# Attention scores by matmuls of 32-row groups in place of zero-padded 104-row ones

## The reference

```
h, hd = 16, 8
q, k, v = x @ Wq, x @ Wk, x @ Wv              # split into 16 heads of 8
log_f = log_sigmoid(x @ Wf);  c = cumsum(log_f)
scores = q k^T * hd**-0.5 + c[i] - c[j]       # causal
out = softmax(scores) @ v;   x += out @ Wo
```

## Time and profile before

| | us |
|---|---|
| median of 3 runs (533.71 to 541.26) | 535.29 |
| span of the profiled execution | 528.3 |
| PE busy, 3680 matmuls | 454.1 (86%) |
| PE weight loads | 320.7 (61%) |
| DVE busy | 377.8 (72%) |
| ACT busy | 278.7 (53%) |
| POOL busy | 148.2 (28%) |

### The profile page before, as it was taken

How to read it: one execution, slowest core, us unless ns; L and a number is a source line. 1 busy time by engine, 2 the same in 40 slices (tenths; PEclk the granted TensorE clock), 3 DMA queues, 4 the chain that set the end, 5 groups by cost and what they waited for, 6 DMA issues and landing times.

```text
span 528.3 us, 12106 instructions
## 1 busy us (share of the span) xinstructions
PE 454.1 (86%) x3680; PEld 320.7 (61%) x3680; DVE 377.8 (72%) x1348; ACT 278.7 (53%) x757; POOL 148.2 (28%) x235
## 2 busy tenths in 40 slices
PE   1788887767989899999999999999999988888884
PEld 1666665554656576576676676676676656666662
DVE  3999999767566576576675675675665654999996
ACT  3477675422445455455455456456355655676663
POOL 8856655421011010110110110110110001556644
PEclk9999999768899999999999999999999999999999
DMA  4210000133322323313312412413312000000101
GB/s 124 80 30 2 1 0 1 63 109 107 101 78 69 110 61 81 113 58 80 115 56 80 115 55 81 117 52 82 115 56 80 5 3 1 20 23 20 40 22 40
DMA packets 30173, 32.31 MB, mean 61 GB/s; under 512 B 3262, under 2 KB 26910, under 8 KB 30140
## 3 DMA queue, kind: packets, MB, share of 16 engines
q1 hardware_dynamic: 30140, 31.92, 21.1%
HBM read 16.05 MB, written 15.20 MB: 59 GB/s over the span
## 4 chain that ended last, share of the span: by engine, by line
PE 33%; DVE 24%; DMA 16%; issue 10%; SPq 8%; POOL 6%; ACT 1%; DVEq 1%; POOLq 0%
DMA a_q_rows<-a_max_t 12%; DVE m_lower L275 6%; PE bank L807 6%; PE bank L790 6%; PE bank L775 6%; SPq L571 4%; PE bank L793 3%; PE bank L778 2%; DVE a_neg_c L757 2%; PE bank L891 2%; POOL a_c_parts L613 2%; DVE a_neg_max L690 2%; POOL a_c_parts L611 2%; DVE x_all L284 2%; DVE m_stats L302 2%
## 5 line engine op out<-in xcount | busy, mean ns | idle before, releaser
L690 DVE TENSOR_REDUCE a_neg_max<-bank 128x2 f32<-128x512 f32 (+1 forms) x192 | 125.5, 686 | 103.5 <-PE bank L778 101.8
L634 ACT ACTIVATE a_weights<-bank 128x512 f32<-128x512 f32 x192 | 105.0, 589 | 82.5 <-PE bank L790 41.2
L775 PE MATMUL bank<-a_k_rows,a_q_rows 104*128 104x256 f32 (+1 forms) x512 | 101.9, 324 | 6.4 <-DMA a_k_rows<-k_stage 6.0
L775 PEld LDWEIGHTS bank<-a_k_rows,a_q_rows 104*128 104x128 f32 x512 | 80.1, 201 | 25.2 <-issue 16.6
L790 PE MATMUL bank<-a_q_rows,a_k_rows 106*128 106x512 f32 x192 | 78.2, 481 | 18.4 <-DMA a_q_rows<-a_max_t 17.1
L238 ACT ACTIVATE m_scaled<-bank,m_gates 128x128 f32<-128x128 f32 x256 | 72.3, 365 | 27.0 <-PE bank L384 27.0
L611 POOL TENSOR_TENSOR a_c_parts<-a_neg_c,a_zero_row 16x256 fp32r<-16x256 f32 x16 | 11.5, 720 | 219.2 <-DVE a_neg_c L757 219.2
L213 POOL TENSOR_TENSOR m_pair<-m_scaled 128x256 f32<-128x256 f32 x64 | 48.3, 755 | 73.0 <-ACT m_scaled L238 72.9
L275 DVE SCALAR_TENSOR_TENSOR m_lower<-bank,m_gates,m_lower 128x128 f32<-128x128 f32 x192 | 65.5, 341 | 1.3
L778 PE MATMUL bank<-a_mask,a_ident 128*128 128x256 bf16 (+1 forms) x192 | 63.3, 330 | 0.0
L807 PE MATMUL bank<-a_weights,a_v 128*32 128x128 f32 x1536 | 62.1, 280 | 0.0
(11 more groups left out here) (118 smaller groups left out, 838.2 us busy)
## 6 DMA issues: line engine op xcount, KB each, us to landing
a_k_rows<-k_stage SPq DMA_DIRECT2D x16, 416.0 KB
k_stage<-a_k_parts SPq DMA_DIRECT2D x48, 128.0 KB
q_stage<-a_q_parts SPq DMA_DIRECT2D x48, 128.0 KB
a_q_rows<-q_stage SPq DMA_DIRECT2D x64, 96.0 KB
x_all<-in_L_attn_x SPq DMA_DIRECT2D x8, 256.0 KB, 2.8
out_x<-x_all SPq DMA_DIRECT2D x8, 256.0 KB, 2.3
a_q_rows<-a_max_t SPq DMA_DIRECT2D x64, 8.0 KB, 2.6
we<-in_L_ffn_We SPq DMA_DIRECT2D x1, 512.0 KB, 4.1
```

Source lines behind the costliest of these rows:

```text
L634: nc.scalar.activation(weights[n // 2 % 3][:, half:half + 4, :].rearrange("p h n -> p (h n)"), wt_bank[n % 2][:, :], ACT.Exp).then_inc(wt_ ...
L690: nc.vector.tensor_reduce(neg_max[:, t, first:first + heads], score_bank[p % 2][:, :].rearrange("p (h n) -> p h n", h=heads), AX.X, ALU.ma ...
L775: nc.tensor.matmul(bank[:, n * keys:(n + 1) * keys], q_rows[b][0:KR, h, t * P:(t + 1) * P], k_rows[b][0:KR, h % NU, 0:keys], start=n == 0, ...
```

## The change

Each group of heads gets its own 32 partitions: rows 32g to 32g+23 the parts, then two of ones (q) or of -c (k), then two for the maxima, 28 in all. `q_rows` shrinks from 106 x 16 x 256 to 128 x 4 x 256 and has no zeros; `set_up_rows` goes. Scores are made for two banks at a time: matmuls of group g into one bank and of group g+1 into the other, in turn, and then the two mask matmuls. Turned scores: each of the six pairs of banks gets 8 matmuls of 128 columns in place of 2 of 512, again in turn between two groups. Both wait for both banks where each bank had its own wait. The k rows are loaded by four DMAs, the maxima are spread over four partitions. `normalise`, `times_v` and `row_max` follow the new order of heads.

```diff
-    ROWS = 3 * HD + 2
-    KR = NG * ROWS
-    KM = KR + 2
+    QR, KR, KM = 3 * HD, 3 * HD + 2, 3 * HD + 4
+    row_group = lambda g, rows: slice(32 * g, 32 * g + rows)
...
-    q_rows = [sb(f"q_rows{b}", [KM, H, N], FP32R) for b in range(3)]
-    k_rows = [sb(f"k_rows{b}", [KM, NU, N], FP32R) for b in range(3)]
+    q_rows = [sb(f"q_rows{b}", [P, NU, N], FP32R) for b in range(3)]
+    k_rows = [sb(f"k_rows{b}", [P, NU, N], FP32R) for b in range(3)]
...
-                sp.dma_start(raw(q_rows[s % 3])[KR + part:KR + part + 1, :, t * P:(t + 1) * P],
+                sp.dma_start(raw(q_rows[s % 3])[KR + part:P:32, :, t * P:(t + 1) * P],
                              raw(max_t[t])[:, part, :]).then_inc(max_in[t], 16)
...
-                sp.dma_start(raw(k_rows[b])[0:KR, :, :], k_dram[b].rearrange("g r u n -> (g r) u n")).then_inc(rows_in, 16)
+                for g in range(NG):
+                    sp.dma_start(raw(k_rows[b])[row_group(g, KR), :, :], k_dram[b, g]).then_inc(rows_in, 16)
...
-    def set_up_rows(pool, b):
-
-        nc.gpsimd.memset(q_rows[b][:, :, :].bitcast(U32), 0).then_inc(zeroed, 1)
...
         def scores(i, s, p):
-            at_least(pe, max_done, i * 12 + p - 1)
...
+            at_least(pe, max_done, i * 12 + p)
+            b = s % 3
+            parts = [score_part(p), score_part(p + 1)]
+            t, keys = int(p >= 4), parts[0][1]
+            for n in range(len(parts[0][2])):
+                for bank, (g, _, heads) in zip(score_bank, parts):
+                    u = heads[n]
+                    nc.tensor.matmul(bank[:, n * keys:(n + 1) * keys], q_rows[b][row_group(g, KR), u, t * P:(t + 1) * P],
+                                     k_rows[b][row_group(g, KR), u, 0:keys], start=n == 0, stop=False, skip_group_check=True)
+            for bank, (_, _, heads) in zip(score_bank, parts):
+                own = bank[:, :].rearrange("p (h n) -> p h n", h=len(heads))[:, :, keys - P:keys]
+                nc.tensor.matmul(own, ident16[:, :], mask16[:, 0:len(heads), :], start=False, stop=True,
+                                 skip_group_check=True).then_inc(scores_ready, 1)
+
+        def turned_scores(i, s, k):
...
+            at_least(pe, wt_exp, i * 12 + 2 * k)
+            b = s % 3
+            t, first, jt = (0, 2 * k, 0) if k < 2 else (1, 2 * ((k - 2) // 2), k % 2)
             diagonal = jt == t
...
+            for u in range(NU):
+                for half in range(2):
+                    rows = row_group(first + half, KM)
+                    last = nc.tensor.matmul(wt_bank[half][:, u * P:(u + 1) * P], k_rows[b][rows, u, jt * P:(jt + 1) * P],
+                                            q_rows[b][rows, u, t * P:(t + 1) * P], start=u == 0, stop=not diagonal,
+                                            skip_group_check=True)
+                    if not diagonal and u == NU - 1:
+                        last.then_inc(wt_ready, 1)
             if diagonal:
-                last = nc.tensor.matmul(bank[:, :], ident16[:, :], mask16_t[:, :, :], start=False, stop=True)
-            last.then_inc(wt_ready, 1)
+                for half in range(2):
+                    nc.tensor.matmul(wt_bank[half][:, :], ident16[:, :], mask16_t[:, :, :], start=False, stop=True,
+                                     skip_group_check=True).then_inc(wt_ready, 1)
```

More of the change, by code:

```diff
@@ L518, in attention_layer @@
     k_stored, q_stored, c_stored, w_ordered = sem("k_stored"), sem("q_stored"), sem("c_stored"), sem("w_ordered")
-    LOADS = NG + 1
+    LOADS = 2 * NG
     raw = lambda tile: tile[(slice(None),) * len(tile.shape)].bitcast(FP32)
     q_dram = nc.dram_tensor("q_stage", (3, NG, 3 * HD, NU, N), FP32, kind="Internal").ap()
-    k_dram = nc.dram_tensor("k_stage", (3, NG, ROWS, NU, N), FP32, kind="Internal").ap()
+    k_dram = nc.dram_tensor("k_stage", (3, NG, KR, NU, N), FP32, kind="Internal").ap()
     f_part = lambda s: 2 if s >= 0 else 3
     def constant_rows(sp):
-        sp.wait_ge(zeroed, 4)
+        sp.wait_ge(zeroed, 1)
         ones = ones_r[:, :].bitcast(FP32).rearrange("r (u n) -> r u n", u=NU)
@@ L532, in constant_rows @@
             for g in range(NG):
-                sp.dma_start(raw(q_rows[b])[ROWS * g + 3 * HD:ROWS * (g + 1), NU * g:NU * (g + 1), :], ones).then_inc(ones_in, 16)
-            sp.dma_start(raw(k_rows[b])[KR:KM, :, :], ones).then_inc(ones_in, 16)
+                sp.dma_start(raw(q_rows[b])[32 * g + QR:32 * g + KR, :, :], ones).then_inc(ones_in, 16)
+                sp.dma_start(raw(k_rows[b])[32 * g + KR:32 * g + KM, :, :], ones).then_inc(ones_in, 16)
     def sync(sp):
@@ L552, in step @@
                 for g in range(NG):
-                    sp.dma_start(raw(q_rows[b])[ROWS * g:ROWS * g + 3 * HD, NU * g:NU * (g + 1), :],
-                                 q_dram[b, g]).then_inc(rows_in, 16)
+                    sp.dma_start(raw(q_rows[b])[row_group(g, QR), :, :], q_dram[b, g]).then_inc(rows_in, 16)
                 wait_apart(sp, k_stored, n * 16 * 3, sp_waited)
                 sp.wait_ge(c_stored, n * 16 * 2)
-                sp.dma_start(raw(k_rows[b])[0:KR, :, :], k_dram[b].rearrange("g r u n -> (g r) u n")).then_inc(rows_in, 16)
+                for g in range(NG):
+                    sp.dma_start(raw(k_rows[b])[row_group(g, KR), :, :], k_dram[b, g]).then_inc(rows_in, 16)
             if 0 <= s < NSEQ:
@@ L688, in row_max @@
             dve.wait_ge(scores_ready, i * 12 + p + 1)
-            t, first, heads = (0, 4 * p, 4) if p < 4 else (1, 2 * (p - 4), 2)
+            pair, half = divmod(p - 4, 4)
+            t, first, heads = (0, 4 * p, 4) if p < 4 else (1, NU * (2 * pair + half % 2) + 2 * (half // 2), 2)
             nc.vector.tensor_reduce(neg_max[:, t, first:first + heads],
@@ L704, in normalise @@
             dve.wait_ge(recip_done, i * 2 + t + 1)
[L705 to L708, removed]
+            nc.vector.tensor_tensor(attn[:, t], out[:, :, 0:HD],
+                                    recip[:, t].unsqueeze(2).broadcast_to([P, H, HD]), ALU.mult).then_inc(attn_done, 1)
         def part(i, s, j):
@@ L767, in tensor @@
     def tensor(pe):
-        def scores(i, s, p):
-            at_least(pe, max_done, i * 12 + p - 1)
[L770 to L779, removed]
@@ L781, in turned_scores, with score_part @@
-        def turned_scores(i, s, n):
-            if n == 0:
+        def score_part(p):
+            if p < 4:
+                return p, P, range(NU)
+            pair, half = divmod(p - 4, 4)
+            return 2 * pair + half % 2, 2 * P, range(2 * (half // 2), 2 * (half // 2) + 2)
+        def scores(i, s, p):
+            at_least(pe, max_done, i * 12 + p)
[11 more added lines that the diff above has]
+                                 skip_group_check=True).then_inc(scores_ready, 1)
@@ L783, in turned_scores @@
+        def turned_scores(i, s, k):
+            if k == 0:
                 pe.wait_ge(max_in[0], (i + 1) * 32)
-            if n == 4:
+            if k == 2:
                 pe.wait_ge(max_in[1], (i + 1) * 32)
-            at_least(pe, wt_exp, i * 12 + n - 1)
-            b, bank = s % 3, wt_bank[n % 2]
-            t, u, jt = (0, n, 0) if n < 4 else (1, (n - 4) // 2, n % 2)
+            at_least(pe, wt_exp, i * 12 + 2 * k)
+            b = s % 3
+            t, first, jt = (0, 2 * k, 0) if k < 2 else (1, 2 * ((k - 2) // 2), k % 2)
@@ L789, in turned_scores @@
             diagonal = jt == t
-            last = nc.tensor.matmul(bank[:, :], k_rows[b][0:KM, u, jt * P:(jt + 1) * P],
-                                    q_rows[b][0:KM, u:H:NU, t * P:(t + 1) * P], start=True, stop=not diagonal)
+            for u in range(NU):
[6 more added lines that the diff above has]
+                        last.then_inc(wt_ready, 1)
@@ L803, in times_v @@
             b, w = s % 3, weights[k % 3]
+            t, first, jt = (0, 2 * k, 0) if k < 2 else (1, 2 * ((k - 2) // 2), k % 2)
             for half in range(2):
[L805 to L808, removed]
+                g = first + half
+                for u in range(NU):
+                    last = nc.tensor.matmul(out_bank[t][32 * u:32 * (u + 1), g * P:(g + 1) * P], v_sb[b][:, jt, NU * g + u, :],
+                                            w[:, 4 * half + u, :], start=jt == 0 and g == 0, stop=jt == t,
+                                            skip_group_check=True)
             last.then_inc(av_done, 1)
@@ L828, in part @@
                 pe.wait_ge(set_up, 2)
-                pe.wait_ge(ones_in, 16 * 3 * (NG + 1))
+                pe.wait_ge(ones_in, 16 * 3 * 2 * NG)
                 pe.wait_ge(before["tiles_done"], 2 * NSEQ)
@@ L836, in part @@
                 scores(i, s, 2 * j)
-                scores(i, s, 2 * j + 1)
             if j == 0 and X:
@@ L863, in part @@
             if X:
-                turned_scores(i - 1, s - 1, 2 * j)
-                turned_scores(i - 1, s - 1, 2 * j + 1)
+                turned_scores(i - 1, s - 1, j)
             if j == 3 and T:
@@ L899, in tensor @@
         return part
```

(5 more changed lines are left out.)

## The result

The changed kernel takes 573.9 us (median of 4 runs, 565.0 to 580.9) against 535.7 before: 1.060 times as long, 95% interval 1.049 to 1.071. The profiled one is that of 565.0 us. Its span of 562.3 is 34.0 us above the span before, which had a mean clock of 0.972.

What follows compares the result with a forecast made beforehand. It took the loop through the slow stage writes to the maxima's landing as bound in steady steps, PE elsewhere. Steps +6.2, filling and emptying +2.0, exp +1, start -0.3 gave +8.9 on 535.3: 544 us, range 525 to 588.

Steps and rivals of the forecast that it cites:

- What bounds the kernel: Steady attention step: stage writes on about four DMA engines delay the maxima, 11.6 us from first stage issue to landing.
- The matmuls: Score and turned-score matmuls: two row groups run side by side, load and stream, saving 2.14 us per step.
- rival B: Row groups don't run side by side, or loads queue: PE grows 4.68 us a step, 595 us; chance 0.24.
- The switches: Changes between 32-row tiles and full-array matmuls: 18 new ones per step at 0.15 us, 2.70 us on PE.
- A: The forecast case: 538 us at 0.10 a switch to 552 at 0.20, PE busy 19.3 a step; chance 0.45.
- Rival C: Not slower: going between 32-row and full matmuls needs no drain, below 0.07 us a switch; 526 us, chance 0.26.
- The loop: Way from one landing of maxima to the next: +0.37 us of PE work, +0.15 for the maxima, +0.52 per step.
- -0.30: Turned scores at k = 2: four rounds replace two 512-column matmuls and a mask moved to k = 3, -0.30 us.
- The 0.15 for them: Maxima DMAs written into four partitions, with more small packets: 0.15 us longer, between 0 and 0.3.
- The double waits, D: Waits for both banks bite: exp or second maximum 0.3 us late in most steps, 550 us; chance 0.05.
- the clock: PE's clock in steady steps: falling below 1.0 would spoil the signs to look for; no price or chance given.
- The sum: Whole kernel: steps +6.2, pipeline filling and emptying +2.0, exp +1, start -0.3, together +8.9 us.

Runs made afterwards that it cites:

- Run 9: Kernel before with q and k columns and DRAM stages reordered so stage writes spread, k rows loaded by four DMAs: 0.940, 504.4 us.
- run 1: Changed kernel's order, counts and double waits, but without 32-row tiles: score matmuls contract over 122 or 124 zero-padded rows; 1.058 of the kernel before, 563.0 us.
- run 6: Changed kernel plus four full-array filling matmuls of 512 columns in part j = 2, before the wait for the maxima: 1.030 of the kernel before, 550.3 us.
- run 7: Changed kernel plus four filling matmuls of 512 columns in the same wait, as 32-row tiles over 24 rows: 1.069 of the kernel before, 576.5 us.
- run 4: Changed kernel without any mask matmul, scores and turned scores unmasked: 1.123 of the kernel before, 599.3 us.
- run 5: Kernel before without any mask matmul, scores and turned scores unmasked: 1.011, 543.2 us.
- run 10: Changed kernel with the DRAM stages reordered so that stage writes spread: 0.984 of the kernel before, 528.9 us.
- run 11: Scores alone tiled in 32-row groups, turned scores padded as before, stage writes spread: 0.930 of the kernel before, 497.6 us.
- run 2: Scores alone tiled as in the change, turned scores one 512-column matmul over padded rows: 1.024 of the kernel before, 548.9 us.

## Why the prediction came out as it did

**What bounds the kernel: right.** The distance from SP's first stage issue to the landing was 11.6 us and is 11.5 now (305.72 to 317.21). Run 9 bears it out.

**The matmuls: right.** Two groups run side by side, loads included: 0.055 a turned matmul, against 0.105 in run 1. So rival B, queued loads at 595 us, is refuted. That a round with 256 keys takes 0.115 is carried over from before: four take 0.43 with the switch, which does not part the two.

**The switches: right in the sum, wrong in the split.** With rounds at the prices of before, entering costs 0.43 - 0.23 = 0.20 and 0.59 - 0.40 = 0.19, where the prediction had 0.15; with the 0.11 a round that the loads' starts show, the second is 0.15. Leaving to a mask costs 0.33 - 0.26 = 0.07 and 0.54 - 0.46 = 0.08, where it had 0.15. A pair is 0.27 against 0.30. PE is busy for 18.9 us of a step, where 19.3 was forecast for A; the terms as measured leave 0.3 us of growth in place of 0.56, the busy time shows 0.14. The rule of the Trainium skill (TensorEngine Tiling (Array Packing), Key Properties), that a change of the tiling mode drains TensorE, fits this trace: time is lost at each change, 0.07 to 0.20 us. That the lost time is a drain, no view shows. Rival C, which needed less than 0.07 a switch, falls: a switch is 0.13 to 0.14 in the mean.

**The loop: right in its sum, by terms that offset each other.** +0.52 a step was forecast, +0.55 to 0.6 measured. From the first turned matmul behind the landing to SP's first stage issue it is 8.95 us (296.77 to 305.72) against 8.25: +0.70 where +0.37 was forecast. The prediction lacked the wait of 0.38 us for x_t. The exponential ahead of x_t on ScalarE starts 0.68 us behind the first turned matmul, 0.54 before, as the two banks fill in turn, while PE comes to the f projection without the mask. So part j = 2 starts that projection at 1.61 us in place of 1.47, and brought none of its -0.30. On the other side the maxima over four partitions cost nothing that shows: 4.82 from issue to landing, 4.87 before. The 0.15 for them was too much, and the distance from the stage issue to the landing even shrank by 0.1.

**The double waits, D: no case.** The step shows no wait for them on PE beyond 0.2 us; the 0.38 us for x_t are another wait.

**What failed is a term of the sum put at zero: the clock.** The sum was +8.9, of which 7 to 8 are in the trace. The other 26 us are clock. The prediction named it only in its last sentence, "The clock falling below 1.0 in steady steps would spoil all of these", and gave it neither price nor chance. The kernel before had reason enough to ask: 0.83 in 100 to 180 us, with PE waiting 1.1 us of every steady step, and the change took full-array streaming out and left that wait. The range held the time since it reached towards B, for a reason that did not hold; so that the time fell inside it is luck. (By its own terms A ends at 550 and not at 552: 12 x 0.77 + 3.5 x 1.46 + 0.7 is 15.)

**Why the clock fell.** Shown: the same number of filling columns holds the clock over 128 rows and not over 24 (runs 6, 7), and at the same busy share matmuls over 122 rows bring no dent where 32-row tiles do (runs 1, 7); taking away full-array masks lowers it to 0.722 with tiles and to 0.897 without (runs 4, 5); with the stage writes spread, no dents come in the steady steps (runs 9 to 11). So tiles that don't hold the clock are one part of it. What the other part is stays open. It is not the wait alone: run 7 waits less than run 10 and has the dents. Full-array work that comes more often, every 19.25 us in run 10 and every 20.5 in the changed kernel, would fit those two, but it doesn't order all the runs: run 2 has more of it than the changed kernel and seven dents to its three. How many dents an execution has varies as well, with clocks of 0.888 to 0.918 for the changed kernel alone. Open too: what sets the 10 to 51 us at half clock at the start of attention, which full-row kernels have as well.

## What to carry to other kernels

Before crediting a saving on TensorE, see whether another resource fixes the step; if so the saving becomes waiting, and a kernel with less work can even be slower by its clock, as in run 5. Price row tiling in three terms: rounds that overlap, 0.15 to 0.2 us for each entry, and full-array work that no longer holds the clock. And read the share of busy DMA engines during a write: 0.27 of 16 is the work of about four engines, and an order of axes whose outer one is long gained more here than any change to the matmuls.

## What the runs showed of the hardware

- Eight 128-column loads and matmuls alternating between two 32-row groups take 0.055 us each (pairs of loads 0.11 apart), 0.105 over all rows.
- Entering 32-row tiles costs 0.15 to 0.20 us, leaving them to a full-array bf16 matmul 0.07 to 0.08.
- Full-array filling of 0.9 us a step took a kernel from 1.060 to 1.030 of the time before (clock 0.918 and 0.909 to 0.954); as many columns in 24-row tiles left it at 1.069 (0.906 to 0.911).
- With PE busy for 0.98 of the time, matmuls over 122 and 124 rows kept full clock in every steady step, while with tiles of 24 to 28 rows it fell to half seven times, for 6.8 us each.
- A stage write whose DRAM side has an outermost axis of 4 ran at 83 GB/s, one of 128 rows in a line at 262 GB/s.
